# The back products of the last feed-forward in half precision: the gelu's values split by GpSimd and VectorE

## The reference, cut to what matters

```python
def _L1_ffn_ref(x, U1, V1, b1, U2, V2, b2):          # x: (4, 1024, 256) f32, layer-normed
    P = jnp.einsum('bsd,dr->bsr', x, U1)              # 256 -> 64
    H = jax.nn.gelu(jnp.einsum('bsr,rf->bsf', P, V1) + b1)   # 64 -> 1024
    Q = jnp.einsum('bsf,fr->bsr', H, U2)              # 1024 -> 64: the "back" products
    return jnp.einsum('bsr,rd->bsd', Q, V2) + b2      # 64 -> 256
x = x + _L1_ffn_ref(_layernorm(x), ...)
```

## Time and profile before

| | us |
|---|---|
| Median of 3 runs (lowest to highest) | 1070.42 (1067.05 to 1070.70) |
| The profiled execution, its own time | 1072.19 |
| Its span, first to last instruction | 1070.2 |
| PE busy in the span | 920.6 (86%) |
| DVE busy | 625.5 (58%) |
| ACT busy | 507.3 (47%) |
| POOL busy | 423.4 (40%) |

### The profile page before, as it was taken

How to read it: one execution, slowest core, us unless ns; L and a number is a source line. 1 busy time by engine, 2 the same in 40 slices (tenths; PEclk the granted TensorE clock), 3 DMA queues, 4 the chain that set the end, 5 groups by cost and what they waited for, 6 DMA issues and landing times. The chain is left out here.

```text
span 1070.2 us, 24472 instructions
## 1 busy us (share of the span) xinstructions
PE 920.6 (86%) x8070; PEld 636.2 (59%) x8070; DVE 625.5 (58%) x1526; ACT 507.3 (47%) x865; POOL 423.4 (40%) x592
## 2 busy tenths in 40 slices
PE   6699999997027999999999999996388888878996
PEld 4455556554026898989889898874123444444552
DVE  3567888875794444444444444433767888646561
ACT  1478888875312333333333323321256766655663
POOL 2287777752102333342212122111865565103451
PEclk9789999999557999999999999998558999999998
DMA  5323434324420212121111112111324221000212
GB/s 178 72 85 105 134 115 135 119 87 149 166 68 21 60 40 61 40 60 41 49 52 45 56 40 61 41 31 60 103 74 103 74 71 59 2 1 2 54 46 60
DMA packets 73729, 75.45 MB, mean 70 GB/s; under 512 B 22730, under 2 KB 66874, under 8 KB 73626
## 3 DMA queue, kind: packets, MB, share of 16 engines
q1 hardware_dynamic: 67146, 56.31, 17.6%
q0 software_dynamic: 6480, 17.70, 6.3%
HBM read 51.64 MB, written 22.34 MB: 69 GB/s over the span
## 5 line engine op out<-in xcount | busy, mean ns | idle before, releaser
L1416 DVE CAST hh_e<-h_e 128x512 f16<-128x512 f32 (+1 forms) x156 | 63.5, 407 | 216.6 <-ACT h_e L1392 139.2
L1340 PE MATMUL up_ps<-xT_e,experts 128*128 128x256 f16 (+1 forms) x624 | 164.5, 264 | 4.1 <-ACT h_e L1392 3.4
L1342 PE MATMUL up_ps<-xT_e,experts 128*128 128x256 f16 (+1 forms) x624 | 164.5, 264 | 0.0
L1341 PE MATMUL up_ps<-xT_e,experts 128*128 128x256 f16 (+1 forms) x624 | 163.7, 263 | 0.0
L1354 PE MATMUL y_ps<-experts,hh_e 128*128 x568 | 154.9, 273 | 1.1 <-DVE hh_e L1418 0.3
L1355 PE MATMUL y_ps<-experts,hh_e 128*128 x568 | 155.0, 273 | 0.0
L1356 PE MATMUL y_ps<-experts,hh_e 128*128 x568 | 154.8, 273 | 0.0
L1270 POOL COPY idx_e<-token 128x2 int32 (+2 forms) x39 | 22.5, 577 | 298.6 <-PE xT_ps_e L1315 249.3
L1392 ACT ACTIVATE h_e<-up_ps 128x512 f32<-128x512 f32 (+1 forms) x156 | 87.2, 559 | 108.3 <-PE up_ps L1342 106.8
L1418 DVE TENSOR_TENSOR hh_e<-h_e,hh_e 128x512 f16<-128x512 f32 (+1 forms) x156 | 100.5, 645 | 5.4
L1676 ACT ACTIVATE prob_a<-sT_ps_a 77x1024 f32<-77x1024 f32 x64 | 64.8, 1015 | 41.3 <-PE sT_ps_a L1580 39.2
(11 more groups left out here) (310 smaller groups left out, 1977.3 us busy)
## 6 DMA issues: line engine op xcount, KB each, us to landing
experts<-in_L_ffn_w SPq DMA_DIRECT2D x22, 512.0 KB, 4.0
y_scratch<-y_e SPq DMA_DIRECT2D x32, 256.0 KB, 3.5
x<-in_x SPq DMA_DIRECT2D x32, 128.0 KB, 3.2
experts<-in_x SPq DMA_DIRECT2D x64, 64.0 KB, 2.4
x_scratch<-x SPq DMA_DIRECT2D x16, 256.0 KB, 2.5
xh_scratch<-xn SPq DMA_DIRECT2D x16, 256.0 KB, 2.8
w_r<-in_L_ffn_w SPq DMA_DIRECT2D x8, 512.0 KB, 4.0
x_a<-x_scratch SPq DMA_DIRECT2D x32, 128.0 KB
```

The costliest lines, as they stand in the source:

```text
L1340: mm(out, w[0], xT[0][:, c, 0:W_], start=c == 0, stop=False)
L1341: mm(out, w[0], xT[1][:, c, 0:W_], start=False, stop=False)
L1342: last = mm(out, w[1], xT[0][:, c, 0:W_], start=False, stop=c == DC - 1)
```

## The change

U2 is split once, in `expand`, into two half-precision parts u2h (scaled by WSCALE = 64). For each step, the gelu's output h (f32) is split too: POOL copies it to half precision (hh[0]), then DVE subtracts that copy from h and writes the rest in half precision (hh[1]). `back` then makes three half-precision products per half of tokens in place of one f32 product, and it waits for DVE's low part instead of ACT's gelu. `second` scales by 1/WSCALE. The gelu now waits for the low part of four steps ago before it overwrites its buffer of h. POOL's and DVE's orders are rewritten so that the splits stand between the other work.

```diff
 # in attend's expand(), on DVE, behind the two instructions that split V1
+                    nc.vector.tensor_scalar(G["u2h"][:, 0, :, :], G["u2"][:, :, :], WSCALE, None, ALU.mult).then_inc(unit.w1h_ok, 1)
+                    dve.wait_ge(unit.w1h_ok, 3)
+                    nc.vector.scalar_tensor_tensor(G["u2h"][:, 1, :, :], G["u2"][:, :, :], WSCALE, G["u2h"][:, 0, :, :],
+                                                   ALU.mult, ALU.subtract).then_inc(unit.w1h_ok, 1)
...
 # feed_forward, @block.gpsimd
-                for n in range(4, NT):
-                    unit_deviation(nc, pool, G, n)
-                    biased(n - 4)
-                for n in range(NT - 4, NT):
-                    biased(n)
+                def hidden(u, m):
+                    j = u * MS + m
+                    pool.wait_ge(h_ok, j + 1)
+                    after(pool, back_done, j - 3)
+                    nc.gpsimd.tensor_copy(hh[0][:, j % 4, :], h[:, j % 4, :]).then_inc(hhi_ok, 1)
+
+                for u in range(UNITS):
+                    for m in range(MS):
+                        hidden(u, m)
+                        if m in (0, 2, 4, 5) and u + 1 < UNITS:
+                            unit_deviation(nc, pool, G, 4 * (u + 1) + (0, 2, 4, 5).index(m))
+                        if m in (1, 3, 6, 7):
+                            biased(4 * u + (1, 3, 6, 7).index(m))
...
 # @block.tensor
-                    pe.wait_ge(h_ok, j + 1)
+                    pe.wait_ge(hlo_ok, j + 1)
                     if m == 0:
                         after(pe, low2_ok, u)
-                    for i in range(2):
-                        last = mm(low2_ps[flat(i, RANK), :], u2[:, m, :], h[:, j % 4, flat(i, U // 2)],
-                                  start=m == 0, stop=m == MS - 1)
+                    for n, (wh, a) in enumerate(((0, 0), (1, 0), (0, 1))):
+                        for i in range(2):
+                            last = mm(low2_ps[flat(i, RANK), :], u2h[:, wh, m, :], hh[a][:, j % 4, flat(i, U // 2)],
+                                      start=m == 0 and n == 0, stop=m == MS - 1 and n == 2)
...
 # @block.scalar, gelu
-                    after(act, back_done, j - 3)
+                    after(act, hlo_ok, j - 3)
...
 # @block.vector
+                def hidden(u, m):
+                    j = u * MS + m
+                    dve.wait_ge(hhi_ok, j + 1)
+                    nc.vector.tensor_tensor(hh[1][:, j % 4, :], h[:, j % 4, :], hh[0][:, j % 4, :], ALU.subtract).then_inc(hlo_ok, 1)
...
                 for u in range(UNITS):
-                    if u + 1 < UNITS:
-                        for n in range(4 * u + 4, 4 * u + 8):
-                            if n + 1 < NT:
-                                rows(n + 1)
-                            normed_rows(n)
-                            if u and n % 4 == 2:
-                                result(u - 1)
+                    more = u + 1 < UNITS
+                    for m in range(MS):
+                        hidden(u, m)
+                        if more and m in (1, 3, 5, 6):
+                            normed_rows(4 * u + 4 + (1, 3, 5, 6).index(m))
+                        if more and m in (0, 2, 4, 6):
+                            n = 4 * u + 5 + m // 2
+                            if n < NT:
+                                rows(n)
+                        if u and m == 4:
+                            result(u - 1)
+                    if more:
                         low(u + 1)
```

More of the change, by code:

```diff
@@ L1882, in allocate_last @@
     G["ff_in"] = L.sem("ff_in")
+    G["u2h"] = L.sb("u2h_f", [P, 2, HID // P, RANK], F16)
     G["f"] = First()
@@ L1902, in feed_forward @@
         h = L.sb("h_f", [P, 4, U])
+        hh = [L.sb(f"hh{i}_f", [P, 4, U], F16) for i in range(2)]
+        u2h = G["u2h"]
+        hhi_ok, hlo_ok = L.sem("hhi_ok_f"), L.sem("hlo_ok_f")
         low2 = L.sb("low2_f", [P, U // 2])
@@ L1966, in first @@
                         if u == 0:
-                            pe.wait_ge(w1h_ok, 2)
+                            pe.wait_ge(w1h_ok, 4)
                     after(pe, h_ok, j - 1)
@@ L2057, in second @@
                     after(dve, out_done, u)
-                    nc.vector.tensor_copy(low2[:, :], low2_ps).then_inc(low2_ok, 1)
+                    nc.vector.tensor_scalar(low2[:, :], low2_ps, 1 / WSCALE, None, ALU.mult).then_inc(low2_ok, 1)
+                def hidden(u, m):
+                    j = u * MS + m
+                    dve.wait_ge(hhi_ok, j + 1)
+                    nc.vector.tensor_tensor(hh[1][:, j % 4, :], h[:, j % 4, :], hh[0][:, j % 4, :], ALU.subtract).then_inc(hlo_ok, 1)
                 def result(u):
@@ L2071, in _ @@
                 for u in range(UNITS):
-                    if u + 1 < UNITS:
-                        for n in range(4 * u + 4, 4 * u + 8):
-                            if n + 1 < NT:
-                                rows(n + 1)
-                            normed_rows(n)
-                            if u and n % 4 == 2:
-                                result(u - 1)
+                    more = u + 1 < UNITS
[10 more added lines that the diff above has]
+                    if more:
                         low(u + 1)
-                    elif u:
-                        result(u - 1)
                     second(u)
```

## The result

The change made the kernel slower: 1171.82 us median (1170.36 to 1173.47) against 1070.56 (1067.05 to 1070.78) for the kernel before beside it, a ratio of 1.0955 with a 95% interval of 1.0933 to 1.0977. That is 101 us more, where 88 were forecast. The profiled execution took 1170.55 us with a span of 1168.0.

A forecast was written before the change was run, and what follows sets the result against it. PE's work bounded the kernel before; the change makes a chain through PE, ACT, POOL and DVE. On 1072.2 us, 65 for seven units, 5 for the last, 1 for U2's split and 17 for the clock gave 1160, range 1128 to 1184.

The forecast's parts named there:

- the round: Last feed-forward: PE, ACT, POOL, DVE and back to PE takes 3.14 us for two steps, four rounds 12.6 us.
- The transposes: In PE's queue, waiting for rows normalised after subtractions 3 and 6: PE stands twice a unit for almost 3 us.
- DVE beside POOL: DVE's subtraction of 0.69 us loses some 0.25 beside POOL's bias add, at steps 1, 3, 6 and 7; bounds 0 and 0.35.
- The clock: Last feed-forward, PE partly at half clock: 3.1 us a unit, 25 over eight units, two thirds taken: 17 us.
- The sum at full clock: One feed-forward unit along its latest waits: 4.74, 4.30, 7.78 and 3.39, together 20.2 us for 10.92.
- The last unit: Last feed-forward unit, without transposes, goes by rounds: 14.5 us against PE's 9.3, so 5 us more.
- The split of U2: Two DVE operations behind V1's split, where PE waits for DVE's attention heads: 1.0 us more, bounds 0 and 1.1.
- The products: PE's `back` takes 0.43 us for 0.58: 0.15 less, 64 times, 9.6 us, won only if PE stayed the bound.
- full clock throughout: Rival: the same stalls in the last feed-forward with the clock never falling, 1143 us; chance 0.20.
- the transposes do not stall: Rival: DVE gets to its rows early enough and only the round counts, 1087 us; chance 0.06.
- the copy is slow: Rival: POOL's copy costs 1.04 us, four on a unit's path, 14 us in all: 1174, or 1182 at half clock; chance 0.09.
- PE stays the bound: Rival: gelu, copy and subtraction hide behind other PE work, so the kernel gets faster, 1063.6 us; chance 0.03.

The follow-up runs named there:

- Rows early: The changed kernel with the next unit's rows normalised in steps 0 to 3 instead of 1, 3, 5 and 6: 1125.22 us, ratio 1.0512.
- PE kept busy: The changed kernel with 20 products of 256 columns put ahead of each pair of transposes, in PE's wait: 1154.16 us, ratio 1.0791.
- firsts ahead and without the bias: firsts ahead with GpSimd's bias add cut to one column, the bias left out for the other 255: 1096.98 us, ratio 1.0254.
- firsts ahead: Rows early, with PE issuing first(u, m + 2) ahead of back(u, m), so three steps in flight: 1115.09 us, ratio 1.0427.

## Why the prediction was right

Forecast 1160 with a range of 1128 to 1184; measured 1171.8. The chain was the forecast's: the stalls at the transposes, the round, the copy and the clock are all there. One term of the sum, the subtraction beside the bias add, was mis-sized beyond its bounds, and one was put at nothing without being named, the normalisation beside a copy. The number lies in the range with some luck: the forecast's own mechanism, with the clock at half throughout, ends at 1168, and the range went above that only for a slow copy, which did not come.

**The transposes.** As forecast: PE stands twice a unit for 3.0 us in front of them (14 waits, 42.4 us), released by the normalisation. Rows early took out 46.6 us, the clock that came back included.

**The hand-overs and the copy.** 1.94 us from a `first` to its subtraction for 1.96; the copy took 609 ns for 0.61.

**DVE beside POOL.** Too small: 0.25 forecast per subtraction, with a bound of 0.35. Measured are 0.35 at step 1 and 0.51 at steps 3, 6 and 7. The step scaled the loss by the time of overlap, and that was its fault. In the timeline above the bias add ends at 1051.67 and the subtraction at 1052.22, 0.55 us later; at 1041.97 to 1042.70 with a subtraction to 1043.25 it is the same 0.55. It is so for all 32: whenever in the add a subtraction begins, it ends 0.55 us behind it, so it loses more the earlier it begins. 0.9 us a unit more than forecast. The normalisation of the earlier trace rows fits this too, with another constant: it ended 0.15 us behind the add (1019.65 against 1019.50), and so lost only 0.17. The Trainium skill says so, in "SBUF — State Buffer", section "SBUF: two separate sides": the shared ports are locked for a whole instruction, and the loser blocks. The trace agrees, and the prediction had weighed only the page that speaks of contention. It agrees for the wide instructions alone: 22 subtractions began beside GpSimd's one-column power, which took 0.55 us, and none was over 0.71.

What decides is which of the two begins first, and the add is not the only one that holds DVE up. In the same unit of the changed kernel a normalisation began just behind a copy:

```profile
1059.83 0.61 POOL L1947 CAST hh_f<-h_f 128x512 f16<-128x512 f32 x1 [1.08 <-ACT h_f L2046]
1059.88 0.71 DVE L1861 TENSOR_SCALAR xh_f<-X,mv_f,rstd_f 128x256 f32<-128x256 f32 x1
```

It ends 0.15 us behind the copy and takes 0.71 for 0.40. Six of the seven units have this, on the path to the second pair of transposes, and there the sum had the plain 0.33.

**The clock.** 17 us forecast, 17.7 by the kernel with PE kept busy, which was not at full clock throughout. The mean unit of the changed kernel is 24.06 us, the unit at full clock 21.37, so 2.7 us a unit for the 2.1 forecast.

**The sum at full clock.** 20.2 us a unit forecast, 21.4 measured at clock 1.00. Of the 1.2, 1.1 is what DVE lost beside GpSimd: in that unit four subtractions and a normalisation were longer by 2.1 us together, where the sum had 1.0.

**The last unit.** 5 us and 2 of clock forecast, 7.3 measured (19.0 for 11.7).

**The split of U2.** 1.0 forecast, 1.5 to 4.7 measured. The wait was right (1.06, and that is the whole cost where the clock stayed full); that the clock could fall behind it was not in the step. In the profiled execution of the changed kernel it cost 5.5 us.

**What makes 101 of 88.** The 88 are counted from the profiled execution, 1072.2; from the median of 1070.6 the forecast is 89 away. The seven unit-to-unit steps took 92.3 us more than before, where 65 and seven eighths of 17, so 79.9, were forecast. Of these 12.4 us, 6.2 are the subtractions (7 x 0.88), 3.9 the clock (7 x 0.56), and of the remaining 2.3 some 1.8 the six normalisations beside a copy (6 x 0.3).

**The products.** 0.15 us each was 0.13, and in the changed kernel it counts for nothing.

Of the rivals, full clock throughout is out: the granted clock moved between both levels all through the stage. That the transposes do not stall, that the copy is slow, and that PE stays the bound are out by the rows above. What stays open is how DVE's remaining queue, GpSimd's and the round share the 14.1 us that a unit takes with firsts ahead and without the bias; DVE is busy for 11.5 of them and GpSimd for 10.2.

## What to carry to other kernels

Before work is taken off the engine that bounds, follow the whole loop that the new hand-over makes, through every queue, with the number of steps in flight: here 3.14 us for two steps, against 0.13 us saved per step. Look at what stands behind each new wait in the queue of its engine; moving four normalisations ahead in DVE's queue took 46.6 of the 101 us back. Where work goes to VectorE and GpSimd at the same time, lay out which wide instructions will run side by side: the one that begins second waits for the other. Where one kind of instruction alternates with another on PE, count the changes of tiling first: pairing them gave 0.6% for an edit of order alone.

## What the runs showed of the hardware

- GpSimd's wide instructions and DVE's subtraction (128x512, two SBUF inputs) or normalisation (128x256, f32) held each other up, and the one that began second paid. Behind GpSimd's add or copy, a subtraction ended 0.54 to 0.55 us after it (1.04 to 1.21 us for 0.69, changed kernel) and a normalisation 0.15 after it (0.71 to 0.74 for 0.40). Behind a subtraction, an add ended 0.58 us after it (1.17 for 0.72) and a copy 0.47 after it (up to 1.07 for 0.61; firsts ahead). Beside GpSimd's one-column operations the subtraction kept its 0.69.
- 20 products put into each of PE's 14 waits for normalised rows made a kernel 17.7 us faster; the granted clock of a unit was 1.00 instead of 0.64.
- A wait that grew from 1.38 to 2.44 us had a spell at the half clock right behind it in eight of ten profiled executions, 6.8 us long in one of them, and none in two.
